# Splitting the keys of a second cross-attention in the feed-forward stage ahead of it, and taking a magnitude in quarters

## The reference

```python
x = x + tanh(g_xattn[0]) * xattn_0(layernorm(x), ctx, mask)   # stage A: one head, 512 wide, masked softmax
x = x + tanh(g_ffn[0])   * ffn_0(layernorm(x), w_up, w_down)  # stage B
x = x + tanh(g_xattn[1]) * xattn_1(layernorm(x), ctx)         # stage C
x = x + tanh(g_ffn[1])   * ffn_1(layernorm(x), w1, w2, w3)    # stage D: silu(x w1) * (x w2) w3

def ffn_0(x, w_up, w_down):                 # weights ternary, activations rounded to 8 bits per token
    h = square(relu(bitlinear(x, w_up)))    # bitlinear: Hadamard transform, rounding, product
    return bitlinear(h, w_down)

def xattn_1(q, y):                          # 16 heads per batch of 32 channels, 1601 keys
    weight = softmax(einsum('bct,bcs->bts', q * s, k * s))    # q and k = v are reshapes of x and ctx
    return einsum('bts,bcs->bct', weight, v)
```

## Time and profile before

| | us |
|---|---|
| median of 3 runs (lowest, highest) | 1832.61 (1830.69, 1837.39) |
| the profiled execution: own time, span | 1832.33, 1830.5 |
| stage A | 0 to 468.4 |
| stage B | 468.4 to 701.2 |
| stage C | 701.2 to 1552 |
| stage D | 1552 to 1830.5 |
| busy: PE, DVE, ACT, POOL | 1610.6, 1184.1, 841.9, 826.7 |
| longest single group: the exponentials of stage C (832) | 531.0 |
| mean granted clock of TensorE, share of full speed | 0.951 |

### The profile page before, as it was taken

The page is one execution under the profiler, slowest core; times in us unless marked ns, Lnnn a source line. Parts: engine busy times, 40 slices in busy tenths (PEclk is TensorE's granted clock), DMA queues, the critical chain, the costliest instruction groups (busy, mean ns, idle before and its releaser), DMA issues. The chain is left out here.

```text
span 1830.5 us, 22118 instructions
## 1 busy us (share of the span) xinstructions
PE 1610.6 (88%) x7540; PEld 614.6 (34%) x7568; DVE 1184.1 (65%) x1538; ACT 841.9 (46%) x1241; POOL 826.7 (45%) x324
## 2 busy tenths in 40 slices
PE   5999999799688886789999999899999996889898
PEld 2444444344334441122222222222222221444443
DVE  3769999887355556677767777677777641443443
ACT  1321221212334442477777777677777775111110
POOL 0022214643112222767778777687777777000000
PEclk9999999899889996799999999999999999899999
DMA  9232223023211113312222222222222241000000
GB/s 325 76 121 78 84 83 106 30 95 119 75 32 26 27 27 93 113 41 59 67 63 72 76 75 75 76 75 51 55 67 67 54 109 32 1 23 0 23 23 23
DMA packets 136395, 124.36 MB, mean 68 GB/s; under 512 B 61774, under 2 KB 112226, under 8 KB 136294
## 3 DMA queue, kind: packets, MB, share of 16 engines
q1 hardware_dynamic: 131302, 112.56, 21.7%
q10 hardware_dynamic: 4992, 10.49, 1.7%
HBM read 73.49 MB, written 10.76 MB: 46 GB/s over the span
## 5 line engine op out<-in xcount | busy, mean ns | idle before, releaser
L1477 ACT ACTIVATE c_prob<-c_scores,ctx_scales 128x512 f32<-128x512 f32 (+1 forms) x832 | 531.0, 684 | 221.1 <-PE c_scores L1533 218.0
L1384 DVE TENSOR_REDUCE c_piece_max<-c_unit 128x1 f32<-128x804 f32 x512 | 488.3, 987 | 208.5 <-PE c_unit L1516 205.2
L1322 POOL TENSOR_TENSOR c_prob_sum<-c_prob_sum,c_prob 128x2048 f32<-128x2048 f32 x96 | 434.8, 4529 | 90.9 <-ACT c_prob L1477 86.9
L1533 PE MATMUL c_scores<-c_queries,c_keys 97*128 97x512 f16 (+1 forms) x832 | 321.4, 392 | 40.6 <-ACT c_prob L1477 33.2
L1516 PE MATMUL c_unit<-c_khigh,c_qdiag 128*128 128x402 f16 x1024 | 274.2, 351 | 44.6 <-DVE c_piece_max L1384 32.7
L1542 PE MATMUL c_out<-c_prob,c_VT 128*32 128x512 f32 (+1 forms) x1664 | 225.0, 613 | 0.1
L1533 PEld LDWEIGHTS c_scores<-c_queries,c_keys 97*128 97x128 f16 (+1 forms) x832 | 80.9, 98 | 369.7 <-ACT c_prob L1477 322.6
L676 PE MATMUL a_S<-a_ctxT,a_xnT 128*128 128x401 f32 x512 | 190.2, 516 | 7.2 <-ACT a_prob L633 3.9
L706 PE MATMUL a_o<-a_ctx,a_probT 128*128 128x512 f32 (+1 forms) x416 | 183.2, 597 | 0.0
L1516 PEld LDWEIGHTS c_unit<-c_khigh,c_qdiag 128*128 128x128 f16 x1024 | 90.5, 100 | 152.5 <-DVE c_piece_max L1384 90.2
L567 ACT COPY a_probT<-a_tp 128x512 f32<-128x512 f32 x48 | 28.0, 585 | 217.8 <-PE a_tp L691 210.8
(11 more groups left out here) (197 smaller groups left out, 1905.8 us busy)
## 6 DMA issues: line engine op xcount, KB each, us to landing
c_k<-in_keys SPq DMA_DIRECT2D x16, 801.0 KB, 6.7
c_keys<-c_khigh SPq DMA_DIRECT2D x128, 100.1 KB, 2.2
a_ctx<-in_ctx SPq DMA_DIRECT2D x12, 1024.0 KB, 7.2
c_VT<-in_values SPq DMA_DIRECT2D x16, 768.0 KB
a_ctxT<-in_ctxT SPq DMA_DIRECT2D x12, 802.0 KB, 4.7
c_keys<-c_krest SPq DMA_DIRECT2D x64, 100.1 KB, 2.2
a_weights<-in_L_ffn_weight SPq DMA_DIRECT2D x3, 1408.0 KB, 14.4
weights_back<-a_weights SPq DMA_DIRECT2D x3, 1408.0 KB, 8.3
```

The source lines that it names most:

```text
L1322: nc.gpsimd.tensor_tensor(psum4[:], a[:], prob[(j * MC + c) % RING][:], ALU.add).then_inc(sums_taken, 2 if i == 1 else 1)
L1384: nc.vector.tensor_reduce(piece_max[j % 2][:, k // 2, k % 2:k % 2 + 1], U[bank(unit)][:, :, 0:PIECE], axis=AX.XY, op=ALU.max).then_inc(uni ...
L1477: nc.scalar.activation(prob[(j * MC + c) % RING][0:w, h, :], STp[h % 2][0:w, :], ACT.Exp, scale=score_scale[0:w]).then_inc(exp_done, 1)
L1533: nc.tensor.matmul(STp[h % 2][0:w, :], K[p][:, h, c * P:c * P + w], Q[p][:, h, :], start=True, stop=True).then_inc(scores_ready, 1)
```

## The change

The keys' two parts are now made in stage B and kept in HBM (`key_parts`). ACT loads a group's keys, casts the scaled keys to f16 in two halves of 801 columns, DVE subtracts in two halves, ACT stores both parts; group g takes four iterations i = 4g to 4g+3 on ACT (KEYS_FROM = 0, KEY_STEPS = 4), and DVE follows two iterations later (RESTS_FROM = 2). In stage C, SP loads the high part where the keys were loaded and stacks the keys from HBM in three DMAs a group instead of twelve within SBUF; ACT's `split_keys` and POOL's `rest_of_k` go. In stage B, DVE scales ahead of `quantize` for stage 2 of the last batch. In stage A, the magnitude is taken in quarters of a batch, at the steps of TOPS_AT, and the bites follow a table of steps, BITES_AT.

```diff
@@ cross_attention_0 @@
-        BITES_FROM, BITES_EACH = 3, 4
+        BITES_AT = {3: 4, 4: 3, 5: 4, 6: 3, 7: 4, 8: 4, 9: 4, 10: 3, 11: 4, 12: 4, 13: 4, 14: 4, 15: 3}
+        TOPS_AT = {0: [0, 1], 1: [2], 3: [3]}
+        for b in range(1, B):
+            TOPS_AT.update({4 * b: [4 * b, 4 * b + 1], 4 * b + 1: [4 * b + 2, 4 * b + 3]})
...
             def load_transposed(b):
-                if b > 0:
-                    sp.wait_ge(ctx_topped, b)
                 for n in range(4):
                     if b > 0:
+                        sp.wait_ge(ctx_topped, (b - 1) * 4 + n + 1)
                         sp.wait_ge(ctxT_free, (b - 1) * 4 + n + 1)
...
-                if k % ST == 2:
-                    context_top(k // ST)
                 if k == 1:
                     block_maxima()
                     layernorm(1)
+                for i in TOPS_AT.get(k, []):
+                    context_top(i)
...
-                if k >= BITES_FROM:
-                    for _ in range(BITES_EACH):
-                        if bites:
-                            bite(*bites.pop(0))
+                for _ in range(BITES_AT.get(k, 0)):
+                    bite(*bites.pop(0))
@@ ffn_0, DVE @@
+            def rest_of_keys(g, half):
+                cols = half_of_keys(half)
+                dve.wait_ge(khigh_ready, 2 * g + half + 1)
+                if g > 1:
+                    dve.wait_ge(k_stored[g % 2], 32 * (g // 2))
+                nc.vector.scalar_tensor_tensor(krest[g % 2][:, cols], kt[g % 2][:, cols], key_scale, khigh[g % 2][:, cols],
+                                               ALU.mult, ALU.subtract).then_inc(krest_ready, 1)
...
-                if pending is not None:
+                alone = v is not None and v[0] == 2 and v[1] == B - 1
+                if pending is not None and not alone:
                     quantize(pending)
                     pending = None
                 if v is not None and v[0] in (0, 2):
                     scale(v)
+                    if pending is not None:
+                        quantize(pending)
                     pending = v
...
+                g, step = divmod(i - RESTS_FROM, KEY_STEPS)
+                if 0 <= g < G and step in (0, 2):
+                    rest_of_keys(g, step // 2)
@@ ffn_0, ACT @@
+            def store_keys(g):
+                act.wait_ge(krest_ready, 2 * g + 2)
+                for part, k in enumerate((khigh, krest)):
+                    act.dma_start(key_parts_dram[part][g], k[g % 2][:]).then_inc(k_stored[g % 2], 16)
+
+            def split_keys(g, half):
+                cols = half_of_keys(half)
+                act.wait_ge(k_loaded[g % 2], 16 * (g // 2 + 1))
+                if g > 1:
+                    act.wait_ge(k_stored[g % 2], 32 * (g // 2))
+                nc.scalar.activation(khigh[g % 2][:, cols], kt[g % 2][:, cols], ACT.Copy, scale=key_scale).then_inc(khigh_ready, 1)
+
+            load_keys(0)
+            load_keys(1)
             normalized(0)
...
+                g, step = divmod(i - KEYS_FROM, KEY_STEPS)
+                if 0 <= g < G and step in (0, 2):
+                    split_keys(g, step // 2)
+                if step == 1 and 1 <= g <= G - 1:
+                    store_keys(g - 1)
+                    if g + 1 < G:
+                        load_keys(g + 1)
+            store_keys(G - 1)
+            for j in range(2):
+                act.wait_ge(k_stored[j], 32 * G // 2)
@@ cross_attention_1, SP @@
-                    for h in range(H):
-                        head = slice(h * CH, (h + 1) * CH)
-                        for part, (k, q) in enumerate(((khigh[o], qhigh[o]), (krest[o], qhigh[o]), (khigh[o], qrest))):
-                            rows = slice(part * CH, (part + 1) * CH)
-                            sp.dma_start(Q[o][rows, h, :], q[head, :]).then_inc(stacked, 16)
-                            sp.dma_start(K[o][rows, h, :], k[head, :]).then_inc(stacked, 16)
+                    for part, (k, q) in enumerate(((0, qhigh[o]), (1, qhigh[o]), (0, qrest))):
+                        rows = slice(part * CH, (part + 1) * CH)
+                        for h in range(H):
+                            sp.dma_start(Q[o][rows, h, :], q[h * CH:(h + 1) * CH, :]).then_inc(stacked, 16)
+                        src = key_parts_dram[k][bass.ds(n, 1), :, :].rearrange("o (h c) m -> c (o h) m", h=H)
+                        sp.dma_start(K[o][rows, :, :], src).then_inc(stacked, 16)
...
                     sp.wait_ge(stacked, (n + 1) * STACKS)
-                if nxt and (not isinstance(n, int) or n + 2 < G):
-                    load_keys(n + 2, o)
                 if more:
+                    if main:
+                        load_keys(g + 2, j % 2)
                     load_diagonal(g + 2, j % 2)
@@ cross_attention_1, ACT: split_keys goes @@
-                nc.scalar.activation(kt[j][:], kt[j][:], ACT.Copy, scale=key_scale).then_inc(kscaled, 1)
-                act.wait_ge(kscaled, n + 1)
-                nc.scalar.copy(khigh[j][:], kt[j][:]).then_inc(khigh_ready, 1)
@@ cross_attention_1, POOL: rest_of_k goes @@
-                nc.gpsimd.tensor_tensor(krest[j][:], kt[j][:], khigh[j][:], ALU.subtract).then_inc(krest_ready, 1)
```

More of the change, by code:

```diff
@@ L473, in bit_scales, with context_top @@
                 nc.vector.reciprocal(bit_recip[:], shared["bit_scales"][:]).then_inc(bit_scales_ready, 1)
[L475 to L481, removed]
+            def context_top(i):
+                b, n = divmod(i, 4)
+                dve.wait_ge(ctxT_loaded[n], 16 * (b + 1))
+                nc.vector.tensor_reduce(ctx_tops[:, i:i + 1], CT[:, :, n * PIECE:(n + 1) * PIECE], axis=AX.XY, op=ALU.max,
+                                        apply_absolute_value=True).then_inc(ctx_topped, 1)
+                if i == 4 * B - 1:
+                    dve.wait_ge(ctx_topped, 4 * B)
+                    nc.vector.tensor_reduce(ctx_tops[:, 4 * B:4 * B + 1], ctx_tops[:, 0:4 * B], axis=AX.X, op=ALU.max).then_inc(ctx_topped, 1)
             def context_scales():
@@ L534, in _ @@
                     bit_scales()
-                if k >= BITES_FROM:
-                    for _ in range(BITES_EACH):
-                        if bites:
-                            bite(*bites.pop(0))
+                for _ in range(BITES_AT.get(k, 0)):
+                    bite(*bites.pop(0))
+            assert not bites
             add_out(K - 2)
             context_scales()
-            for n, m in bites:
-                bite(n, m)
             add_out(K - 1)
@@ L772, in ffn_0 @@
         gg = [sb(f"b_gg{j}", [P, I]) for j in range(2)]
+        G, MK = keys_dram.shape[0], keys_dram.shape[2]
+        KEYS_FROM, KEY_STEPS = 0, 4
+        RESTS_FROM = KEYS_FROM + 2
+        key_scale = shared["ctx_scales"][:, 0:1]
+        kt = [sb(f"b_k{j}", [P, MK]) for j in range(2)]
+        khigh = [sb(f"b_khigh{j}", [P, MK], F16) for j in range(2)]
+        krest = [sb(f"b_krest{j}", [P, MK], F16) for j in range(2)]
         Q = 2 * B * ST
@@ L793, in ffn_0 @@
         turned = {(stage, t): sem(f"b_turned{stage}_{t}") for stage in (1, 3) for t in range(ST)}
+        k_loaded = [sem(f"b_k_loaded{j}") for j in range(2)]
+        khigh_ready = sem("b_khigh_ready")
+        krest_ready = sem("b_krest_ready")
+        k_stored = [sem(f"b_k_stored{j}") for j in range(2)]
         y_full = sem("b_y_full")
@@ L821, in width, with half_of_keys @@
             return D if u[0] in (0, 3) else I
+        def half_of_keys(half):
+            return slice(half * MK // 2, (half + 1) * MK // 2)
         block = stack.enter_context(nc.Block())
@@ L998, in rise, with load_keys @@
                 nc.scalar.square(sq[k % 2][:], sq[k % 2][:]).then_inc(sq_ready, 1)
+            def load_keys(g):
+                act.dma_start(kt[g % 2][:], keys_dram[g]).then_inc(k_loaded[g % 2], 16)
+            def store_keys(g):
[10 more added lines that the diff above has]
+            load_keys(1)
             normalized(0)
@@ L1093, in cross_attention_1 @@
         TB = D // P
-        MK = keys_dram.shape[2]
+        MK = key_parts_dram[0].shape[2]
         PIECE = 402
@@ L1229, in load_keys @@
             def load_keys(n, j):
-                sp.dma_start(kt[j][:], keys_dram[bass.ds(n, 1), :, :].rearrange("o p s -> p (o s)")).then_inc(k_loaded[j], 16)
+                if not isinstance(n, int) or n > 1:
+                    sp.wait_ge(unit_full, FULL0 + place(n - 2, PAIRS - 1) + 1)
+                sp.dma_start(khigh[j][:], key_parts_dram[0][bass.ds(n, 1), :, :].rearrange("o p s -> p (o s)")).then_inc(k_loaded[j], 16)
             def load_values(n, j):
@@ L1299, in rest_of_q @@
                 nc.gpsimd.tensor_tensor(qrest[:], xn[:], qhigh[j][:], ALU.subtract).then_inc(qrest_ready, 1)
-            def rest_of_k(n, j):
-                pool.wait_ge(khigh_ready, n + 1)
-                wait(pool, stacked, (n - 1) * STACKS)
-                nc.gpsimd.tensor_tensor(krest[j][:], kt[j][:], khigh[j][:], ALU.subtract).then_inc(krest_ready, 1)
```

(15 more changed lines are left out.)

27 lines of the change are left out of this document (8 added, 19 removed).

## The result

Over four runs each on one chip the changed kernel took 1872.01 us (median; 1862.56 to 1874.71), the kernel before 1831.65 (1827.78 to 1837.39): ratio 1.0209, 95% interval 1.0162 to 1.0255; that it is slower is clear of the noise, that it is by 2% or more is not. The profiled execution took 1869.75 us (span 1868.0), 37.4 more than that of before.

What follows compares the result with a forecast made beforehand. PE was taken as the bound, so edits count only where they open or close holes in its row. Stage A +46, B +24 and C -29 gave +41 against the profiled execution, so 1873 us, range 1840 to 1897.

Steps and rivals of the forecast that it cites:

- the table (44 + 4): Stage A: the new bite table ends pieces later, so ACT's stores hold PE, 44 us, plus 4 at the lower clock.
- it enters 1.1 late: Stage A, step 9: DVE starts 1.1 us late because the step before carries 26.2 us of work; part of a 10.3 stall.
- the quarters (-2): Stage A: magnitude in quarters ends the maximum's lateness in steps 7 and 11, worth -2 us (0 to -6).
- loads (12): Stage B: key loads land late at batch changes and ACT stands at the cast, 4 us a batch, +12 (0 to +16).
- issues (2): Stage B: ACT's store issues, three in a row ahead of a copy in the chain, cost +2 us (0 to +4).
- tail (3.5): Stage B's end: the last half's subtraction and two stores end the stage later, +3.5 us (0 to +6).
- order (-1): Stage B, last batch: scale ahead of quantise takes ACT's move off DVE's path, -1 us (+1 to -2).
- DVE's subtractions at 0: Stage B: 32 DVE operations of 1.1 us each fit in DVE's idle time, 0 (bounds 0 and +6).
- ten half-casts of 0.8 = +8: Stage B: three casts in each batch's ACT-DVE chain and one at the first batch's start cost +8; the others are hidden.
- The waits: Stage C: PE's waits for exponentials behind ACT's key passes go, 13 x 1.86 + 0.96 = -25.1 us.
- The term for the clock: Stage C: with the stalls gone PE spends less time at the lower clock, -4 us (0 to -6.6).
- POOL and SP had slack, so their part is 0: Stage C: removing POOL's rest of 3.2 us and nine of 24 DMA issues a group gains nothing, 0.

Runs made afterwards that it cites:

- a_quarters: The kernel before with only the context's magnitude taken in quarters of a batch, old bite table kept; 1820.70 us, ratio 0.9925.
- b_sp_queue: The changed kernel with a third key buffer, loads issued a group earlier, and key loads and stores issued by SP instead of ACT; 1862.67 us, ratio 1.0151.
- c_halves: The kernel before with ACT's scale and cast passes over the keys in stage C taken in halves, four pieces between exponentials; 1810.60 us, ratio 0.9877.
- b_off_chain: b_sp_queue with four buffers and 24 of 32 half-casts moved to where stage-3 and stage-1 units alternate, eight in iterations 2 to 9; 1855.74 us, ratio 1.0117.
- c_diag_early: c_halves with SP's load of the next diagonal issued ahead of the values' and keys' loads and the wait for the stacks; 1795.65 us, ratio 0.9793.
- b_off_small: b_off_chain with DVE's subtractions cut to 8 columns from the fifth group on; 1851.90 us, ratio 1.0091.

## Why the prediction was right

It forecast 1873 (1840 to 1897) and slower; the median was 1872. By stage it said +46, +24, -29, 0; measured +48, +29, -35, -5 (first to first statistics). The closeness of the sum is partly luck: B came out 5 above its forecast, C 6 and D 5 below. The range had an error too: its parts' lower ends, 34 + 8 - 33, add to +9, not to +28 (which is 34 + 8 - 14). The lower end of 1840 that was set is hardly under 1833 + 9.

- **Stage A, the table (44 + 4).** Right in mechanism, and nearly in size as long as it is counted with the quarters, against the kernel before. Waits forecast at 10.3, 18.8 (12.6 + 6.2), 14.1 and 17.5; measured 14.3, 18.5, 13.7 and 17.5. (The closing paragraph of the prediction says 25 for the second; that does not follow from its own terms, and the sum never used it.) The 4 us in step 10 come from one mis-sized term, "it enters 1.1 late": the maximum of step 9 starts at 269.50 with R at 264.43, 5.07 late. Two rows on DVE and two on POOL in the changed kernel say why:

```profile
227.51 5.56 DVE L435 TENSOR_SCALAR a_neg<-a_weights 128x2816 bf16<-128x2816 bf16 x1 [0.22 <-DVE a_picked L457]
232.99 5.59 DVE L435 TENSOR_SCALAR a_pos<-a_weights 128x2816 bf16<-128x2816 bf16 x1
```

```profile
227.43 4.90 POOL L360 TENSOR_TENSOR a_weights<-a_picked,a_deq 128x2816 bf16<-128x2816 bf16 x1 [25.05 <-DVEq L459]
232.28 5.56 POOL L356 TENSOR_TENSOR a_weights<-a_weights,a_srecip 128x2816 bf16<-128x2816 bf16 x1
```

  Such a DVE operation takes 0.88 us alone. Started within 0.1 us behind POOL's weighing, and then while POOL scaled, each took about as long as POOL's: 11.15 for the two. With the old table the piece ended with the step, maximum and addition stood next, and only one of the two was caught (5.47 at 223.27 before). The new table runs on into the next piece at once. The Trainium skill's page "SBUF — State Buffer", section "Who interferes with whom", has this as a rule: a tensor_scalar in DVE's two-port mode and a GpSimd operation shut each other out for the whole instruction. The rows agree; my forecast had weighed only the rule's case of two inputs.
- **Stage A, the quarters (-2).** Alone they are worth 12.2, shown by a_quarters. I had put the 4.3 of step 12 and the 4.28 of step 16 into the table's existing waits, so the sum held (60.6 - 12.2 = 48.4 against 46), but the step as a statement on the edit was wrong, by 10 us, and with it the price of the table alone, by 12.6. The late maximum shifted the bites behind it, and so the clip of step 16: the maximum of step 15 starts at 440.61 before with R15 at 436.61, and at 430.93 with R15 at 430.98 in a_quarters, where the sixth weighing comes 4.8 us earlier against R15.
- **Stage B, loads (12), issues (2), tail (3.5), order (-1).** Measured 8.3, some 7 (1.7 in B's length, as a new wait takes 4.9 back), 3.5 (the last addition stands 4.9 before B's end against 1.4) and -2.5. DVE's subtractions at 0: shown twice, but for the first groups.
- **Stage B, "ten half-casts of 0.8 = +8": mis-sized.** 29.4 - 8.3 - 1.7 - 3.5 + 2.5 leaves 18.4, of which 4.9 are b_sp_queue's late store, so about 13.5 for the casts and the clock; this is by subtraction, as no run took the casts alone away. A cast took 957 ns; half the pass of the earlier trace rows was too low. In c_halves a scaled pass over 801 columns takes 960 ns, over 1602 it took 1627, so some 290 ns of each is fixed, and for the cast without a scale (859 and 1528) 190. The Trainium skill's page "ScalarE: Activation LUTs", section "What ACT_TABLE_LOAD costs", gives 186 ns + 0.833 ns a column with 93 ns more for a per-partition scale, an estimate of 0.95 us for this cast; the rows agree. Two claims were wrong beside it. That the stage-3 and stage-1 phase hides casts: b_off_chain puts 24 there, loses 4.5 and 3.3 us in its first two, and at the end of the third batch is 2.8 us behind b_sp_queue. And that the first batch's start has one cast in the chain, 0.8: ACT's copies are 3.8 us late by iteration 10 in the changed kernel, and still 3.2 in b_sp_queue. How the 13.5 us split among these is open. And PE's busy time in B rose by 7.4 us with a granted clock of 0.89 against 0.91, for which I had no term (eight of the 832 matmul records were missing before, a part of it).
- **Stage C.** The waits: 25.1 forecast, 33.2 - 8.1 = 25.1 measured; ACT's rows of output taking are mostly 47.1 to 47.2 us apart, forecast 47.2, 49.0 or more before. The term for the clock was too small: PE's busy time fell by 8.8 us, I had 4 (bound 6.6). "POOL and SP had slack, so their part is 0" was wrong for SP: with the stall gone, the diagonal was next late by 13.8 us in all (c_halves). The change takes nine issues off SP's queue (0.63 each, 5.7 us a group) and halves the bytes of the keys' load ahead of the diagonal, which then lands 2.8 us after its issue (median) instead of 5.0. Something of this was needed for the 25 us; no run tells the issues from the bytes. The right sum hid this. For POOL the claim held: c_diag_early keeps its subtraction.
- **Stage D (0).** 277.7 before, 272.7 after; in all the kernels it lay between 272.1 and 277.8, and at 277.7 to 277.8 in just the three whose C still had the old stalls.

## What to carry to other kernels

When work comes in pieces that a second engine finishes and a third hands on in program order, it matters in which step the last bite of a piece falls, not how even the load is; and put a store that waits for another engine behind what the critical engine needs, then look at what ends the stage. Before moving work to another stage because it comes in one lump, cut the lump: here four pieces between exponentials, and one DMA issued earlier, gave 33.9 of the 35.3 us in that stage and cost nothing in the stage ahead. When a stall is taken away, read the queue of the engine that issues DMAs for what lands within that stall's length of its use.

## What the runs showed of the hardware that I had not expected

- A fixed part of 190 to 290 ns in each ACT pass (above), which makes halves dearer: 30.5 us for 32 halves against 26.0 for 16 wholes.
- POOL's butterfly (L893) took 1423 ns on average in b_off_chain, where DVE subtracts beside it, 1268 in b_off_small with 8 columns from the fifth group on, and 1266 in the kernel before (L859). Contention is there, but B was as long.
- The granted clock of the untouched stage D: in the kernel before PE ran at the lower level (1.2 of 2.4 GHz) for 31.9 us of D, in the changed one for 20.1, and D was 5.0 us shorter. Whether the code ahead of it decides that, and how, was not settled.
